# Decoder layer on one core: inputs laid out on the host, a new beginning, and the second norm's rows turned behind an out projection

## The reference

```python
x = layernorm(x + attention(x))        # 16 query heads, 4 key/value heads, D = 128, rotary, window of 128 keys back
x = layernorm(x + cross(x, ctx))       # query = ctx Wq + bq, key = ctx Wk + bk, softmax(query key^T), x_m = x attention
x = layernorm(x + moe(x))              # 2 shared + 16 routed experts of width 176, top 4 by sigmoid gates
```

## Time and profile before

| | |
|---|---|
| median of 3 runs | 410.21 us (409.89 to 410.97) |
| the profiled execution, its own time | 410.56 us |
| its span in the trace | 408.8 us |
| PE busy | 95% of the span |
| DVE, ACT, POOL busy | 70%, 65%, 44% |
| mean granted clock of PE | 0.991 |
| HBM read | 26.8 MB |

### The profile page before, as it was taken

One profiled execution on the slowest core, in us unless ns is written; L12 is line 12 of the kernel. 1 busy time (PEld: TensorE's weight loads), 2 busy tenths in 40 slices (PEclk: granted clock), 3 DMA queues, 4 the chain that ended last, 5 costly groups with the idle time before them and its releaser, 6 DMA issues.

```text
span 408.8 us, 8464 instructions
## 1 busy us (share of the span) xinstructions
PE 389.0 (95%) x2559; PEld 347.4 (85%) x2559; DVE 284.2 (70%) x796; ACT 267.1 (65%) x670; POOL 180.1 (44%) x314
## 2 busy tenths in 40 slices
PE   6976999999998999999999999999999999999995
PEld 3666898998897999888999878889989998999994
DVE  2785999786786876867787877477659545744445
ACT  3666998776767785866776787565775743444352
POOL 0243766455564743663563675486956300000000
PEclk9996999999999999999999999999999999999999
DMA  6711330000001000000000099322222212243221
GB/s 202 270 53 53 108 124 27 2 2 2 1 2 26 0 0 0 0 0 0 0 0 0 0 261 329 109 79 88 88 85 82 96 59 78 82 152 97 91 64 51
DMA packets 24677, 28.25 MB, mean 69 GB/s; under 512 B 2961, under 2 KB 17194, under 8 KB 24650
## 3 DMA queue, kind: packets, MB, share of 16 engines
q1 hardware_dynamic: 24650, 27.92, 21.6%
HBM read 26.80 MB, written 1.11 MB: 68 GB/s over the span
## 4 chain that ended last, share of the span: by engine, by line
PE 72%; DVE 10%; ACT 7%; issue 5%; POOL 2%; DMA 1%; SPq 1%; DVEq 0%; ACTq 0%; POOLq 0%
PE bank L704 20%; PE bank L706 19%; PE bank L705 19%; PE bank L834 4%; PE bank L843 3%; PE bank L833 2%; PE bank L806 2%; PE bank L800 1%; ACT probs L1091 1%; ACT xln L1100 1%; DVE by_sin L1349 1%; DMA ctx_sb<-in_ctx 1%; DVE pT_lo L1228 1%; DVE by_cos L1348 1%; ACT probs L1089 1%
## 5 line engine op out<-in xcount | busy, mean ns | idle before, releaser
L1022 ACT ACTIVATE hid<-bank,b_cols 128x512 f32<-128x512 f32 x48 | 33.0, 687 | 55.6 <-PE bank L706 47.0
L1245 DVE TENSOR_TENSOR hid<-hid,gate_rows 128x512 f32<-128x512 f32 (+1 forms) x44 | 31.8, 724 | 48.0 <-ACT hid L1022 47.8
L1601 POOL TENSOR_SCALAR nprobs<-probs,rsums 128x128 f32<-128x128 f32 x64 | 24.1, 376 | 76.2 <-DVE rsums L1364 67.8
L705 PE MATMUL bank<-w_lo,hid_hi 128*128 128x256 f32 (+1 forms) x200 | 56.3, 282 | 0.0
L1593 POOL TENSOR_TENSOR queryT<-by_cos,by_sin 128x512 f32<-128x512 f32 x32 | 41.1, 1285 | 26.5 <-DVE by_sin L1349 25.5
L1082 ACT COPY swapped<-bank 64x512 f32<-64x512 f32 x40 | 23.3, 583 | 33.7 <-PE bank L706 33.4
L1228 DVE TENSOR_TENSOR hid_lo<-hid,hid_hi 128x512 fp32r<-128x512 f32 x48 | 36.2, 753 | 5.4 <-ACT hid_hi L1043 5.4
L704 PE MATMUL bank<-xT_hi,wq_hi 128*128 128x256 f32 x128 | 38.4, 300 | 1.4 <-issue 1.2
L705 PEld LDWEIGHTS bank<-w_lo,hid_hi 128*128 128x128 f32 (+1 forms) x200 | 37.7, 188 | 2.1
L706 PE MATMUL bank<-x2T_hi,w_lo 128*128 128x512 f32 (+1 forms) x100 | 39.4, 394 | 0.0
L834 PE MATMUL bank<-keyT,queryT 128*128 128x256 f32 x128 | 38.7, 384 | 0.0
(11 more groups left out here) (177 smaller groups left out, 1239.9 us busy)
## 6 DMA issues: line engine op xcount, KB each, us to landing
gate_rows<-gates_d SPq DMA_DIRECT2D x16, 256.0 KB, 3.1
stage<-in_L_attn_q_kernel SPq DMA_DIRECT2D x4, 512.0 KB, 6.5
stage<-in_L_attn_out_kernel SPq DMA_DIRECT2D x4, 512.0 KB, 3.6
w_raw<-in_L_ffn_routed_w SPq DMA_DIRECT2D x2, 1024.0 KB, 9.5
gate_rows<-gates_d SPq DMA_DIRECT2D x8, 224.0 KB, 3.1
gate_rows<-gates_d SPq DMA_DIRECT2D x8, 192.0 KB, 2.8
gate_rows<-gates_d SPq DMA_DIRECT2D x8, 160.0 KB, 2.5
w_raw<-in_L_ffn_routed_w SPq DMA_DIRECT2D x2, 528.0 KB, 8.0
```

The lines of the kernel that those rows point to most:

```text
L705: nc.tensor.matmul(o, sh, ml, start=False, stop=False, **kw)
L1022: nc.scalar.activation(hid[:, u % 2, :], z_bank[u % 3][:], ACT.Relu, bias=b1_cols[:, i % NC:i % NC + 1]).then_inc(relu_done, 1)
L1245: nc.vector.tensor_tensor(own, own, gate_rows[rows, i % 3, :], ALU.mult).then_inc(gated, 1)
L1601: nc.gpsimd.tensor_scalar(nprobs[:, u, 0:W], probs[:, u, 0:W], rsums[:, u, 0:1], 1.0, ALU.mult, ALU.mult)
```

## The change

The host now lays inputs out: the tokens with features on the partitions (`xt`), the cross layer's weights, biases and `ctx` already turned and in one array (`cross`), the experts' weights and centroids as the kernel's tiles want them (`w1`, `w2`), biases in columns (`small`), the three tables in one array. So the transposes of tokens, of `ctx`, of the cross weights, of centroids and biases go, and many small DMAs become a few. The slots `x0` and `x1` become a cast on ACT (`split_x`) and a subtraction on POOL (`x_low`) for the whole block. In block 0 the cross layer's projections and three of the four energies come ahead of `q0`, `e_norm` moves from DVE to POOL, the low part of the second piece of `wq` too, and the `attT` transposes are spread. `y` moves from place 29.25 to 29.35.

```diff
-SLOT_AT = {"x0": -2.5, "x1": -2.5, "q0": -1.25, "k0": -1, "q1": -0.75, "q2": -0.5, "q3": 1.75,
+SLOT_AT = {"q0": -1.25, "k0": -1, "q1": -0.75, "q2": -0.5, "q3": 1.75,
            "k1": 2.75, "q4": 4.75, "v1": 5.5, "v0": 6.5, "q5": 7.25, "q6": 7.75, "q7": 11,
-           "n": 25.5, "m0": 26.5, "m1": 26.75, "y": 29.25}
+           "n": 25.5, "m0": 26.5, "m1": 26.75, "y": 29.35}
...
-    "act": {"slot": 0, "exp": 0.75, "probs_hi": 3, "heads_hi0": 7.25, "heads_hi1": 9.25,
+    "act": {"x": -2.5, "slot": 0, "exp": 0.75, "probs_hi": 3, "heads_hi0": 7.25, "heads_hi1": 9.25,
...
-    "pool": {"slot": 0, "normalise": 0.5, "norm 1": 22.75, "norm 2": 26.75, "keep": 28.75},
+    "pool": {"x": -2.45, "slot": 0, "normalise": 0.5, "norm 1": 22.75, "norm 2": 26.75, "keep": 28.75},
...
-PIECE_AT = dict(zip(PIECE_NAMES, (-2.1, -2.05, -0.9, 2.2, 3.1, 5.4, 6.6, 8.1, 10.1, 12.1)))
+PIECE_AT = dict(zip(PIECE_NAMES, (-2.1, -2.05, -1.6, 2.2, 3.1, 5.4, 6.6, 8.1, 10.1, 12.1)))
+POOL_PIECES = ["q1"]
...
+    "pe": {"cross 0": -2.6, "cross 1": -2.4, "energy 0": -2.3, "energy 1": -2.25, "energy 2": -2.2,
+           "energy 3": -0.7, "attT 0": 1.2, "attT 1": 2.2, "attT 2": 3.3, "attT 3": 4.2},
...
+    "pool": {"e_norm 0": -0.4, "e_norm 1": 0.9, "e_norm 2": 1.9, "e_norm 3": 2.9},
...
-            sp.dma_start(xb[:], x[0].rearrange("(t p) c -> p t c", p=P)).then_inc(ld_xb, 16)
-            sp.dma_start(ident[:], ident_c).then_inc(ld_ident, 16)
...
+            sp.dma_start(cross_sb[:, 0:tokens_0], cross_in[:, 0:tokens_0]).then_inc(ld_cross[0], 16)
+            sp.dma_start(xraw[:].rearrange("p k t -> p (k t)"), xt[0]).then_inc(ld_xt, 16)
+            sp.dma_start(cross_sb[:, tokens_0:], cross_in[:, tokens_0:]).then_inc(ld_cross[1], 16)
...
-                if kind == "x":
-                    e.wait_ge(ld_xb, 16 * (b + 1))
-                    for t in range(TT):
-                        mm = nc.tensor.transpose(o[:, t * P:(t + 1) * P], xb[:, t, j * P:(j + 1) * P], ident[:])
...
-                    e.wait_ge(emptied, slot_count(b, "x1"))
+                    e.wait_ge(x_done, b + 1)
...
+            def split_x(b, _):
+
+                e.wait_ge(ld_xt, 16 * (b + 1))
+                if not (isinstance(b, int) and b == 0):
+                    e.wait_ge(projected, NSLOT * b - len(LATE))
+                nc.scalar.copy(xT_hi[:], xraw[:]).then_inc(x_hi_done, 1)
...
+            def x_low(b, _):
+                e.wait_ge(x_hi_done, b + 1)
+                nc.gpsimd.tensor_tensor(xT_lo[:], xraw[:], xT_hi[:].bitcast(F32), ALU.subtract).then_inc(x_done, 1)
+
+            def once(work, of):
+                if work == "piece":
+                    e.wait_ge(w_hi, of + 1)
...
+                c = int(work[-1])
+                e.wait_ge(dve, place("dve", f"e_rsum {c}"))
+                for t in range(TT):
+                    ins = nc.gpsimd.tensor_scalar(e_exp[:, c, t, :], e_exp[:, c, t, :], e_rsum[:, c, t:t + 1], 1.0,
+                                                  ALU.mult, ALU.mult)
+                ins.then_inc(e_normed, 1)
```

More of the change, by code:

```diff
@@ L95 @@
 NROPE = len(ROPES)
-SPLITS = [s for s in SLOTS if s[0] in "xv"]
+SPLITS = [s for s in SLOTS if s[0] == "v"]
 NSPLIT = len(SPLITS)
@@ L147, in window_order @@
     turns += [(at, "once", name, 0) for name, at in ONCE_AT[engine].items()]
-    if engine in ("act", "dve"):
-        turns += [(at, "once", "piece", PIECE_NAMES.index(name)) for name, at in PIECE_AT.items()]
+    turns += [(PIECE_AT[name], "once", "piece", PIECE_NAMES.index(name)) for name in PIECES_OF[engine]]
     return [(window, work, of) for _, window, work, of in sorted(turns, key=lambda e: e[0])]
@@ L644, in _ @@
[L644 to L653 removed]
+            sp.wait_ge(projected, max(slot_count(B - 1, s) for s in SLOTS if s[0] in "kqv"))
@@ L837, in turn @@
             def turn(b, h):
+                if isinstance(b, int) and b == 0 and h < 2:
+                    after("act", f"e_exp {E_BANK.index(4 + h)}")
                 if isinstance(b, int) and b == 0 and h == 0:
-                    after("act", "attT 3")
+                    e.wait_ge(ld_ident, 16)
                 e.wait_ge(norm_done, head_count(b, h))
@@ L850, in values @@
                 e.wait_ge(emptied, slot_count(b, LAST_V))
+                if isinstance(b, int) and b == 0 and g == 0 and blk == 0:
+                    after("act", "attT 2")
                 if not is_last(b, g, blk):
@@ L1128, in once @@
                     piece(of)
[L1129 to L1138 removed]
+                elif work[:-2] == "cross":
+                    h = int(work[-1])
+                    after(f"xp 0 {h}")
+                    step(nc.scalar.activation(xqT[:, h * HALF:(h + 1) * HALF], bank[4 + h][:], ACT.Identity,
+                                              bias=xb_cols[:, 0:1]), f"xqT {h}")
                 elif work[:-2] == "e_exp":
@@ L1145, in once @@
                     step(ins, work)
-                elif work == "small turned":
-                    after("smallT")
-                    nc.scalar.copy(centT[:].rearrange("p k r -> p (k r)"), bank[7][:, 0:KC * NR])
-                    step(nc.scalar.copy(b1_cols[:], bank[7][:, 64:64 + NC]), "smallT")
                 else:
@@ L1152, in once @@
                     after(work)
-                    step(nc.scalar.copy(attT[:, c, :, :].rearrange("p k r -> p (k r)"), bank[E_BANK[c]][:]), work)
+                    step(nc.scalar.copy(attT[:, c, :, :].rearrange("p k r -> p (k r)"), bank[A_BANK[c]][:]), work)
             for s in (exp_done, pT_hi_done):
@@ L1170, in _ @@
             probs_hi(z, 11)
+            e.wait_ge(ld_small, 16)
             top_out(0)
@@ L1444, in once @@
                     after_act(f"e_exp {c}")
-                    step(nc.vector.reciprocal(e_rsum[:, c, :], e_sum[:, c, :]), f"e_rsum {c}")
-                    settle()
-                    for t in range(TT):
-                        ins = nc.vector.tensor_scalar(e_exp[:, c, t, :], e_exp[:, c, t, :], e_rsum[:, c, t:t + 1], None,
-                                                      ALU.mult)
-                    step(ins, work)
+                    step(nc.vector.reciprocal(e_rsum[:, c, :], e_sum[:, c, :]), work)
             for s in (score_read, rsum_done, pT_done):
```

316 lines of the change are left out of this document (119 added, 197 removed).

## The result

The changed kernel takes 423.8 us (median of 4 runs, 422.1 to 425.6) beside 410.3 us for the kernel before (4 runs, 409.9 to 411.0): 1.033 times as long, 95% interval 1.028 to 1.038. The profiled execution took 422.67 us with a span of 420.6, against 410.56 and 408.8.

What follows compares the result with a forecast made beforehand. PE, busy 389 of 408.8 us, bounds the kernel: time is won or lost where it waits or its clock falls. 410.56 - 3.0 + 8.5 + 5.5 = 421.6, or 421.5 beside a median of 410.2; range 413.5 to 425.5.

Steps and rivals of the forecast that it cites:

- Edges, +8.5: At three block edges `q0` waits for POOL's `x_low` behind head 13's division: 2.5, 3.0 and 3.0 us later.
- Clock, +5.5: PE's clock falls after idle gaps at block edges: 2.2 us at each long gap, 1.1 at the first.
- rival (a): At the block edges the clock stays up, so only the edges' 8.5 us are paid: 416 us, chance 0.2.
- (c): Clock falls at all three edges, 2.5 us each, and the beginning brings only 2: 425 us, chance 0.15.
- Beginning, -3.0: Block 0, up to `q4`: earlier cross projections and `q0`, then POOL's divisions, gain 3.0 us, bounds 2 to 5.
- `y`, counted with the edges: At the edges with `y`, its 0.68 us wait for the norm goes; it ends 0.7 us later, casts following.
- End of the loop, 0: After the last block, `y` comes 0.8 us later on PE, but ACT's chain sets what follows: 0.
- Experts' loads, 0: Experts' loads run under attention's last heads, and the experts' matmuls have few waits: 0.

Runs made afterwards that it cites:

- The filled waits: Changed kernel with four useless PE matmuls ahead of the wait for the tokens' low part at each of three block edges: 420.9 us, 1.024 times before.
- the last two kernels: Changed kernel with next block's tokens split a window earlier and `e_exp` divisions on DVE: 403.5 us; the same with the tokens' low part on DVE: 402.2 us.
- the last run: Changed kernel with tokens split a window earlier, `e_exp` divisions on DVE, and the tokens' low part on DVE behind `q7`'s rotation: 402.2 us, 0.980 times before.

## Why the prediction was right, and what was off

The forecast was 421.5, the time is 423.8; the profiled execution, against which the sum was made, was forecast at 421.6 and took 422.67. The mechanism was right, and one term was not.

- **Edges, +8.5.** Measured 7.5 in the profiled execution (2.2 + 2.5 + 2.8 for 2.5 + 3.0 + 3.0). The chain ran as laid out: cast, DVE's two low parts, score, reciprocal, head 13's division, `x_low`, `q0`. The subtraction took 1.26, where the rotation's 1.30 had been taken. PE's waits were 3.01, 4.64 and 4.65, where gaps of 3.2 and twice 5.1 were laid out.
- **Clock, +5.5.** Measured 4.1 in the profiled execution: 2.5 and 1.6 for 2.2 each, and none at the first edge for 1.1. It is not a constant: in the run with `y` back it fell at all three, at up to 2.7 us each, and a wait of 2.24 us brought it down twice and left it up twice in two runs. The filled waits show that rival (a), no fall, was wrong; (c) was near in its number (425), but not by its mechanism, since the clock fell at two edges. The evidence weighed against (a), that a gap of 1.9 us sufficed once, was read too simply: in the kernel before, PE waited 1.65 us, worked for 0.65 and then waited 1.91, and the clock had left its full level early in that second wait (0.85 over 32 to 33 us, 0.50 over 33 to 34).
- **Beginning, -3.0.** Measured 0 at `v1`, and this is the step that failed: "behind it POOL alternates divisions with heads and rotations and ends the last one at 36.2 at best". It ended at 39.3, and `q4` started at 40.16 for the 36.8 to 38.3 forecast. I had laid POOL's work end to end, and not asked whether head 1's division could start: it hung on an exponential and a reciprocal behind `q3`, which PE issued behind `attT` 0, so POOL idled for 4.68 us with ready work behind. The longer waits also brought the clock down a second time, which the term left out. `q0` itself was 1.6 us earlier (11.46), close to the 1.8 forecast. With that order changed the beginning brings 6.3 us, more than any bound that I gave.
- **`y`, counted with the edges.** That its wait of 0.7 would go and its casts come later was right, and in the changed kernel its place matters little (1.2 us). I missed that the number also moves `y` behind the heads on DVE, which alone costs the kernel before 2.7 us (415.1 to 412.3).
- **End of the loop, 0.** Measured 0.3: the routing of the last block waits 1.1 us for the later `x2T_lo`. **Experts' loads, 0:** PE has no wait on them.

So -3.0 + 8.5 + 5.5 = 11.0 stands beside 0 + 7.5 + 4.1 + 0.3 = 11.9. The total came out close by luck in part: the errors of its terms, +3.0 at the beginning and -2.4 at edges and clock, mostly offset each other. What isn't settled is how often the clock falls after a given wait, and how much it takes (3.0 us at the first edge left it up in the changed kernel and brought it down in two of the other runs): the changed kernel's runs spread over 3.5 us, those of the last two kernels with a full clock over 0.3.

## What to carry to other kernels

When work is moved to an engine that runs in a written order, ask of each entry ahead of it when it can start, and not only how long it takes: moving the work to the faster engine instead brought at most about 1 us more here, while three places ahead of waiting entries brought over 13. An entry whose inputs come early and whose reader is PE goes ahead of entries that hang on PE. And a new wait of PE should be priced with lost clock on top, as a risk and not as a constant: where the clock fell behind an edge in these runs, it cost 1.0 to 2.7 us from `q0` on, and the shortest wait ahead of such a fall was 2.24 us.

## What the runs showed of the hardware

- **DVE and POOL hold each other up.** The subtraction of 128x512 from two SBUF tensors took 0.68 on DVE at the edge, where POOL was idle, and 1.51 in the first window of the last run, where POOL's rotation had started 0.3 us earlier:

```profile
57.94 1.27 POOL L1520 TENSOR_TENSOR queryT<-by_cos,by_sin 128x512 f32<-128x512 f32 x1 [0.62 <-DVE by_sin L1275]
```

  It ended at 59.75, 0.54 behind the rotation's end at 59.21. The low part just before it on DVE, which reads one of its inputs from PSUM, took its usual 0.54 beside the same rotation. POOL's 128x256 division, 0.48 by itself, took 1.45 beside DVE's low part of a weight piece (1.30 from 35.68) in the run with the reordered divisions (from 35.88). The Trainium skill, SBUF — State Buffer, section "SBUF: two separate sides", says that a GpSimd operation that reads SBUF and a DVE operation with two SBUF inputs exclude each other from a shared pair of ports for the whole instruction; these rows agree.
- **A factor of nearly two.** The same subtraction took 1.26 us on POOL and 0.68 on DVE, 1.9 times as long on POOL. The Trainium skill, GPSIMD Engine Reference, section 4.1, which the prediction weighed, says about twice, and these rows agree; but the experiments show that this factor isn't what the change lost its time to.
- **The clock fell after short waits.** In two runs, 2.24 us of idle PE was followed by the lower level at two edges (0.58 over the following 4 us at one, 0.67 over 182 to 186 us at the other) and by the full clock at two others. What decides between them is open.
